# Retention stage: TensorE's order regrouped, rotation's partition swap by DMA, q's row scale in the clip bounds

## The reference

```
q = xf @ Wq.T;  k = xf @ Wk.T * SCALING;  vr = xf @ Wv.T        # 8 heads of 32
qr = q * cos + rotate_every_two(q) * sin;  kr the same with k
# rotate_every_two: (x0, x1, x2, x3, ..) -> (-x1, x0, -x3, x2, ..)
qk = einsum('bhqd,bhkd->bhqk', qr, kr) * mask[None]
den = clip(abs(qk).sum(-1, keepdims=True), 1.0, 50000.0)
out = einsum('bhqk,bhkd->bhqd', qk / den, vr)
out = (out - mu) / sqrt(var + LN_EPS) * ln_g + ln_b             # over each head's 32 values
out = gelu(out, approximate=False) @ Wo.T
```

## Time and profile before

| | before |
|---|---|
| time, median of 3 runs | 2666.49 us (2666.29 to 2668.53) |
| span of the profiled execution | 2667.7 us (its own time is not recorded apart from its span) |
| retention stage within it | about 0 to 1157 us, in which PE is busy 99 to 100% between 170 and 1050 us |
| attention, experts | about 1157 to 1554 us, 1554 to 2668 us |
| DVE, ACT in the stage | about 75% and 60% busy |

### The profile page before, as it was taken

How to read it: one execution, slowest core, us unless ns; L and a number is a source line. 1 busy time by engine, 2 the same in 40 slices (tenths; PEclk the granted TensorE clock), 3 DMA queues, 4 the chain that set the end, 5 groups by cost and what they waited for, 6 DMA issues and landing times. The chain is left out here.

```text
span 2667.7 us, 43895 instructions
## 1 busy us (share of the span) xinstructions
PE 2586.6 (97%) x15328; PEld 1732.6 (65%) x15328; DVE 1844.4 (69%) x2847; ACT 1459.4 (55%) x2044; POOL 517.1 (19%) x444
## 2 busy tenths in 40 slices
PE   5999999999999999969999969999999999999999
PEld 2333343333333434349999958888888888888888
DVE  3877777777777777747777658666666666666665
ACT  2665656565656565635666635555555555555554
POOL 2333333333333333211121210000000000000000
PEclk8999999999999999989999979999999999999999
DMA  6122222222232222121222224000000000000000
GB/s 230 47 77 58 76 68 59 80 55 82 56 84 57 77 58 68 48 85 64 95 94 75 98 90 143 25 25 24 24 24 24 24 24 24 24 24 24 24 17 16
DMA packets 116786, 157.95 MB, mean 59 GB/s; under 512 B 16272, under 2 KB 82328, under 8 KB 116384
## 3 DMA queue, kind: packets, MB, share of 16 engines
q1 hardware_dynamic: 116640, 156.01, 19.7%
HBM read 72.03 MB, written 33.59 MB: 40 GB/s over the span
## 5 line engine op out<-in xcount | busy, mean ns | idle before, releaser
L499 DVE TENSOR_TENSOR l_prod<-l_scores,l_window 128x1024 f32<-128x1024 f32 x512 | 624.0, 1220 | 211.4 <-PE l_scores L325 199.1
L690 ACT ACTIVATE l_absp<-l_prod 128x1024 f32<-128x1024 f32 x512 | 536.5, 1056 | 333.1 <-DVE l_prod L499 331.9
L1707 ACT ACTIVATE e_r<-e_h,e_bn,e_rs 128x512 f32<-128x512 f32 x512 | 399.0, 780 | 484.9 <-PE e_h L1558 480.7
L325 PE MATMUL l_scores<-l_qst,l_kst 96*128 96x512 f32 x1024 | 412.9, 484 | 15.4 <-DMA l_qst<-l_lo 11.6
L325 PEld LDWEIGHTS l_scores<-l_qst,l_kst 96*128 96x128 f32 x1024 | 168.1, 191 | 240.2 <-issue 180.2
L1558 PE MATMUL e_y<-e_whi,e_h2lo 128*128 128x256 f32 x1024 | 289.8, 283 | 0.0
L1557 PE MATMUL e_y<-e_wlo,e_h2hi 128*128 128x256 f32 x1024 | 289.7, 283 | 0.0
L1556 PE MATMUL e_y<-e_whi,e_h2hi 128*128 128x256 f32 x1024 | 289.2, 282 | 0.1
L339 PE MATMUL l_num<-l_prod,l_v 128*32 128x512 f32 x2048 | 273.5, 605 | 0.0
L350 PE MATMUL l_den<-l_absp,l_ones 128*32 128x512 f32 x2048 | 272.7, 604 | 0.0
L1802 DVE CAST e_h1hi<-e_r 128x512 fp32r<-128x512 f32 x256 | 111.2, 434 | 224.3 <-ACT e_r L1707 220.2
(11 more groups left out here) (191 smaller groups left out, 4447.0 us busy)
## 6 DMA issues: line engine op xcount, KB each, us to landing
l_kst<-l_hi SPq DMA_DIRECT2D x256, 64.0 KB, 2.0
l_qst<-l_hi SPq DMA_DIRECT2D x256, 64.0 KB, 2.0
l_raw<-in_xT SPq DMA_DIRECT2D x8, 1024.0 KB, 5.3
l_kst<-l_lo SPq DMA_DIRECT2D x128, 64.0 KB, 2.0
l_qst<-l_lo SPq DMA_DIRECT2D x128, 64.0 KB, 2.0
l_xo<-in_x SPq DMA_DIRECT2D x32, 256.0 KB, 2.8
x_scratch<-l_xo SPq DMA_DIRECT2D x32, 256.0 KB, 2.2
l_xr<-x_scratch SPq DMA_DIRECT2D x8, 1024.0 KB, 8.0
```

The lines of the kernel that those rows point to most:

```text
L325: mm = nc.tensor.matmul(sc[j][:, s, :], kst[g][0:96, h, 128 * kt:128 * kt + 128], qst[c][0:96, h, :], start=True, stop=True)
L499: nc.vector.tensor_tensor(prod[n % 4][:], sc[j][:], win[:, 4 * g + 2 * j:4 * g + 2 * j + 2, w0:w0 + QC], ALU.mult).then_inc(prod_ready, 1)
L690: nc.scalar.activation(absp[n % 4][:], prod[n % 4][:], ACT.Abs).then_inc(abs_ready, 1)
L1707: nc.scalar.activation(r[m][:], p[m][:], ACT.Relu, bias=bn_[layer][1][:, m, e:e + 1], scale=rs[layer][:, m, e:e + 1]).then_inc(done, 1)
```

## The change

1. **PE's order.** A step was: scores pair 0, `sums(i - 1)`, tasks of part 0, scores pair 1, `weighted(i)`, tasks of part 1. It becomes: pair 0, tasks 0, pair 1, tasks 1, `sums(i - 1)`, `weighted(i)`. The matmuls are the same ones.
2. **The swap.** DVE's 64 shuffles go. SP copies `t1` to `t2` with the partitions swapped, by two DMAs of 64 partitions by 2 KB each (`swap_pairs`), which stand ahead of each stack in SP's list. `rotate_sin` (DVE) and `rotate_cos` (POOL) wait for both to have landed.
3. **The row factor of q** is left out of q; the denominator's clip bounds 1 and 50000 are divided by it instead (a table `bounds`, one value per token and head), and `take_den` on DVE becomes two small operations (max, then min). PE waits for the first of them where it waited for the one.
4. **q out of PSUM by ACT** (`take`, at kt = 1 behind ACT's absolutes), not by DVE.

```diff
+            def swap_pairs(n):
+
+                sp.wait_ge(t1_ready, n + 1)
+                for d in range(2):
+                    sp.dma_start(t2[d:128:2, :], t1[1 - d:128:2, :]).then_inc(shuffled, 16)
...
                 if not first:
                     store_x(0, b - 1, 0, 4 * b - 3)
                     load_x(0, b - 1, QC, 16 * (2 * b - 1))
+                swap_pairs(prep_order("q0", b))
                 stack(prep_order("q0", b), qst[1][:, :, :], QUADS["q"], q_stacked)
                 if not first:
                     store_x(1, b - 1, 256, 4 * b - 2)
                     load_x(1, b - 1, QC + 256, 16 * (2 * b - 1))
+                swap_pairs(prep_order("k0", b))
                 stack(prep_order("k0", b), kst[1][:, :, 0:QC], QUADS["k"], k_stacked[0])
...
                 if not last:
+                    swap_pairs(prep_order("k2", b))
                     stack(prep_order("k2", b), kst[0][:, :, 0:QC], QUADS["k"], k_stacked[0])
                 for n in range(2):
                     load_x(n, b, 256 * n, None if first else 32 * b)
                 if not last:
+                    swap_pairs(prep_order("q3", b))
                     stack(prep_order("q3", b), qst[0][:, :, :], QUADS["q"], q_stacked)
...
                     if more:
                         scores(nb, ni, 0)
+                    tasks(0)
+                    if more:
+                        scores(nb, ni, 1)
+                    tasks(1)
                     if i > 0:
                         sums(b, i - 1, first)
                     elif not first:
                         sums(b - 1, STEPS - 1, False)
...
-                    if more:
-                        scores(nb, ni, 1)
                     weighted(b, i, first)
...
-            def q_rotate_in(n, a, g, c):
...
             def rotate_sin(n, c):
 
-                dve.wait_ge(shuffled, n + 1)
+                dve.wait_ge(shuffled, SHUFFLE * (n + 1))
...
-                nc.vector.tensor_scalar(dent[:], nT_A[:, :, 0], 1.0, 50000.0, ALU.max, ALU.min).then_inc(den_ready, 1)
+                nc.vector.tensor_tensor(dent[:], nT_A[:, :, 0], bounds[:, 0, p, :], ALU.max).then_inc(den_floor, 1)
+                dve.wait_ge(den_floor, phase + 1)
+                nc.vector.tensor_tensor(dent[:], dent[:], bounds[:, 1, p, :], ALU.min).then_inc(den_ready, 1)
...
+                    if kt == 1 and (p < 3 or not last):
+                        take(prep_order(f"q{p}", b), A(f"q{p}"), 1.0)
```

More of the change, by code:

```diff
@@ L18, with layer0 @@
 F32R = mybir.dt.float32r
-def layer0(nc, x, xT, wqT, wkT, wvT, woT, lng, lnb, window, rowscale, cosT, sinT, avg8, ident, x1):
+def layer0(nc, x, xT, wqT, wkT, wvT, woT, lng, lnb, window, clip, cosT, sinT, avg8, ident, x1):
     B, L, E = x.shape
@@ L76, in layer0 @@
         win = sb("window", [128, H, (2 * ROWS - 4) * 32])
-        rsc = sb("rowscale", [128, 2, ROWS])
+        bounds = sb("clip", [128, 2, PHASES, 16])
         cos_sb, sin_sb = sb("cos", [128, L]), sb("sin", [128, L])
@@ L144, in _ @@
                 sp.dma_start(dst, src).then_inc(weights_in, 16)
-            for dst, src in ((sin_sb[:], sinT), (cos_sb[:], cosT), (rsc[:], rowscale)):
+            for dst, src in ((sin_sb[:], sinT), (cos_sb[:], cosT), (bounds[:], clip)):
                 sp.dma_start(dst, src).then_inc(tables_in, 16)
@@ L242, in a_free @@
                 else:
-                    pe.wait_ge(den_ready, 4 * b if before == "dT3'" else 4 * b + int(before[2]) + 1)
+                    pe.wait_ge(den_floor, 4 * b if before == "dT3'" else 4 * b + int(before[2]) + 1)
             def b_free(name, b, first, last):
@@ L410, in body @@
[L410 to L419, removed]
@@ L431, in body @@
[L431 to L439, removed]
@@ L440, in body @@
[L440 to L447, removed]
+                    weighted(b, i, first)
@@ L600, in body @@
                     products(b, i, 0, first)
-                    if kt == 2 and prep_q:
-                        shuffle(nq)
                     if kt == 3 and post:
-                        take_den(A("dT" + tag))
+                        take_den(A("dT" + tag), ph, 3 if prev else p - 1)
                         head_sums(Bn("nT" + tag))
-                    if kt == (7 if p == 2 else 6) and prep_k:
-                        shuffle(nk)
                     if not last:
@@ L655, in _ @@
             centre(4 * B - 1)
-            take_den(a_order("dT3'", B - 1, False, "after"))
+            take_den(a_order("dT3'", B - 1, False, "after"), 4 * B - 1, 3)
             variance(4 * B - 1)
@@ L663, in _, with take @@
         def _(act):
-            def k_take(n, a):
+            def take(n, a, scale):
                 if not isinstance(n, int) or n > 0:
@@ L669, in k_take @@
                 act.wait_ge(a_ready, a + 1)
-                nc.scalar.activation(t1[:], pA[:], ACT.Copy, scale=SCALING).then_inc(t1_ready, 1)
+                nc.scalar.activation(t1[:], pA[:], ACT.Copy, scale=scale).then_inc(t1_ready, 1)
             def high(n, before, count):
@@ L746, in body @@
                         if kt == (6 if p == 2 else 5):
-                            k_take(prep_order(f"k{p}", b), A(f"k{p}"))
+                            take(prep_order(f"k{p}", b), A(f"k{p}"), SCALING)
                         if kt == 7:
@@ L1903, in shape_constants @@
     window = gamma[None, :, None, None] ** dist * factor[None, :, None, :]
-    rowscale = np.stack([factor[4 * g + np.arange(128) // 32] for g in range(2)], 1)
+    tok, t, head = np.arange(128)[:, None, None], np.arange(4)[None, :, None], np.arange(4)[None, None, :]
+    scale = np.stack([factor[4 * (p // 2) + head, (512 * (p % 2) + 128 * t + tok) // R].reshape(128, 16) for p in range(4)], 1)
+    clip = np.stack([1.0 / scale, 50000.0 / scale], 1)
     angle = np.repeat(1.0 / 10000.0 ** np.linspace(0.0, 1.0, 16), 2)
@@ L1910, in shape_constants @@
     out = {
-        "window": window.reshape(128, H, -1), "rowscale": rowscale, "cosT": np.tile(np.cos(turn), (4, 1)),
+        "window": window.reshape(128, H, -1), "clip": clip, "cosT": np.tile(np.cos(turn), (4, 1)),
         "sinT": np.tile(sine, (4, 1)), "avg8": np.kron(np.eye(16), np.full((8, 8), 1 / 8)), "ident": np.eye(128),
```

81 lines of the change are left out of this document (43 added, 38 removed).

## The result

The changed kernel takes 2824.83 us (median of 4 runs, 2818.30 to 2828.81) against 2667.51 for the kernel before on the same chip (4 runs, 2666.29 to 2669.76): a ratio of 1.0585, 95% interval 1.0567 to 1.0603, so 157 us slower. The profiled execution has a span of 2821.1 us. PE's last transposes of the retention stage start at 1310.99 us where they started at 1157.15, and from there to the end it is 1510.1 us (before 1510.6), so 153.8 us were lost in the retention stage.

The account below looks back on a forecast made before the run. PE, busy 129.7 of 130 us, was taken to bound the retention stage. Savings of 84 us against waits, start and clock loss summed to +126 on 2667.7, giving 2794; the forecast median was 2792 us, range 2700 to 2860.

Parts of the forecast that it names:

- PE's order with DVE's small waits: Retention stage: fewer changes between full array and narrow groups save 84 us over 256 steps; DVE's extra work returns 12.
- parts 3 and 4: Row factor in the clip bounds and q's exit by ACT: worth nothing by themselves, since DVE is not the bound.
- q3: Phase 3: q3's swap waits behind k2's stack and two loads on SP, costing 7.6 us in seven batches, +53.
- q0 and k0: Phase 0: swaps wait on SP behind stack, loads, store and its wait; q0 +55 (bounds 35 and 65), k0 +12.
- q1, q2, k1 to k3: Other swaps landing late: +14 us for q1 and q2, +4 for k1, k2, k3 and batch 0.
- start: Stage start: swaps and stacks go in series, and batch 0's q0 swap stands behind loads: +12 us (bounds 6 and 18).
- the clock, at q3 and q0: PE's clock halves after long idle waits, 3.4 us on each of 14 waits: +48 us (bounds 0 and 70).
- The step 2.99: PE's step without tasks in the retention stage shrinks from 3.32 to 2.99 us, saving 0.33 each.
- The give-back: DVE's variance, statistics or normalising exceeds its 0.4 us margin, 0.4 us on each of 32 phases: +12 (bounds 0 and 25).
- L + 4.1: PE may start pair 1 of its step 3 4.1 us after L, the swap's landing, once DVE's operations are done.
- the row of 64 KB: Profile row: 2.0 us from a DMA's issue to landing for 64 KB, used for the swap's 128 KB DMAs.
- Rival (a): The stalls come but PE's clock stays up: the forecast without the clock's 48 us, 2744 us; chance 0.25.

Follow-up runs that it names:

- e1: The kernel before with only PE's new order; shuffle, q's exit by DVE and the row factor stay: 2622.60 us, ratio 0.9835.
- e3: The changed kernel with the shuffle kept on DVE, so all of the change but the swap by DMA: 2639.90 us, ratio 0.9895.
- e6: The kernel before with PE's new order and the clip bounds (two-operation `take_den`); shuffle and q's exit on DVE: 2623.65 us, ratio 0.9828.
- e5: The changed kernel with q's exit from PSUM back on DVE at its old place, swap still by SP: 2805.56 us, ratio 1.0513.
- e7: The changed kernel with q0's and q3's swaps moved earlier in SP's list, ahead of loads, store or stack: 2747.94 us, ratio 1.0299.
- e8: The changed kernel with 24 more zero-weight matmuls keeping PE busy in the long waits of phases 3 and 0: 2801.79 us, ratio 1.0493.
- e11: The changed kernel with 48 two-column zero-weight matmuls in phase 0 alone, shifting PE's later instructions by 96: 2813.93 us, ratio 1.0541.
- the best placement: The changed kernel with q's exit on DVE, part 1's tasks last in a step, and q0's, k0's and q3's swaps first: 2700.66 us, ratio 1.0121.

## Why the prediction was right, and where it was not

The forecast was 2792 in a range of 2700 to 2860, and its main chain is shown: SP works in order, q3's and q0's swaps stand behind stacks, loads and a store, DVE waits, then PE. Of the +154 of the stage, its terms measured are:

| term of the sum | forecast | measured, and from what |
|---|---|---|
| PE's order with DVE's small waits | -72 | -45 (e1) |
| parts 3 and 4 | 0 | +17 (e3 less e1) |
| q3 | +53 | 56: phase 3 is 8.0 longer than in e3, 64 over eight, less 8 of the clock |
| q0 and k0 | +67 | 52: phase 0 is 8.8 longer, 62 over seven, less 9 to 10 of the clock |
| q1, q2, k1 to k3 | +18 | 40: phases 1 and 2 are 4.1 and 0.9 longer, eight of each |
| start | +12 | 16 (92.1 less 76.2) |
| the clock, at q3 and q0 | +48 | at most about 17 |
| sum | +126 | about +153 |

**The step 2.99** was exact, and the 0.33 per step real: the narrow groups do lose their extra time beside each other. The Trainium skill, "TensorEngine Tiling (Array Packing)", section "Key Properties", says that changing the tiling mode drains TensorE; the trace agrees, with 0.33 to 0.34 us for each pair of changes taken away. **The give-back** was put down to DVE's variance and statistics, 12 us. It was 39: group means and phase 3's transposes, which wait for `pA` now ahead of the narrow groups (some 17 and 9), and the loop's jump (some 8), read from e1's steps; the rest is spread. I had moved those tasks without asking what they wait for.

**Part 4** was costed at nothing, and there a step failed. I reckoned `t1` ready at 7.0 and it was at 7.5 (650.1 in a phase that began at 642.66), which is near, but I did not ask who wants `pA` next. The transposes of `den` do, and wait in each phase:

```profile
649.56 0.58 ACT L655 ACTIVATE l_t<-l_bankA 128x512 f32<-128x512 f32 x1
```

```profile
650.20 0.66 PE L309 MATMUL l_bankA<-l_ident,l_tB 128*128 128x128 f32 x4 [1.19 <-ACT l_t L655]
```

The step is 4.75 in place of 3.86 in phases 0 to 2, and 5.26 in place of 5.13 in phase 3. e3 less e1 is 17 us and e3 less e6 16. e5's 19 are no third witness, since 15 of them lie in phase 1 beside a fetch that is gone. **The second operation of `take_den`** was put at 0.2 us, in a step where PE has other work. It takes 1.1 to 1.3 in 30 of 32 phases, because POOL's addition runs beside it once the rotation is late (last section), and it stands on the path from the swap to PE, between the sine product and the product that frees pair 1:

```profile
661.79 1.26 DVE L515 TENSOR_TENSOR l_den_t<-l_den_t,l_clip 128x16 f32<-128x16 f32 x1
```

```profile
664.84 1.22 PE L343 MATMUL l_scores<-l_qst,l_kst 96*128 96x512 f32 x2 [0.18 <-DVE l_prod L491]
```

I had put PE's pair 1 at L + 4.1, and it is at L + 5.0 (659.84 to 664.84), in all seven phases 3. That is 0.9 us more on a wait than forecast; no run in the new order has the late swap and this operation at its 0.18 us, so what it costs by itself is not shown.

**q3 and q0**: the forecast landed q3's swap 16.5 us into the phase; it landed at 17.2 (659.84 less 642.66). e7 shows the places in SP's list as the cause. For q0 and k0 the forecast was too high: in batches 1 to 6 the step of q0's wait is 7.8 us longer than in e3 and k0's 1.1, so about 45 us with the clock off where I had 55, and 8 where I had 12.

**q1 and k1**: my 2.05 us for a landing holds where nothing comes between, in e8 and e11 to the tenth; with a fetch of instructions in between it is 3.4 to 4.2. Without the fetch phase 1 is 3.0 us shorter, 24 in all, and the rest of this term, about 16, is near its forecast of 18. So the row of 64 KB was a fair measure of 128 KB, the 2.3 us set beside it in the prediction was 0.2 too high, and the 2.4 in the changed kernel's profile is a median over disturbed and undisturbed ones.

**The clock** was the term most wrong. Half-clock stretches are there as foretold (661.7 to 668.5 at 0.66), but they cost little, since DVE has four products and more to catch up and holds PE anyway: pair 1 starts 5.0 us behind the sine product at half clock here, and at full clock in e7 and e8 too. From the sine product to the next `weighted` are 7.42 us in every undisturbed place at full clock (q3 in e7), 8.5 on average at q3 and 8.7 at q0 after the change: 1.1 and 1.3 us each, not 3.4. Even that is an upper value, since e8 took most of the half clock away and phases 0 and 3 hardly changed. That the sum came near is in part luck: five terms (PE's order, parts 3 and 4, q3, the small waits, the start) were together 73 us too low, and two (q0 and k0, the clock) 46 too high. Rival (a), 2744, was the better on the clock and worse in the sum.

## What to carry to other kernels

Before a copy is handed from an engine that has slack to a queue that works in order, write down what stands ahead of it in that queue at each place: 0.75 us of DVE work a time, on an engine with slack, became 90 us in all in the best placement and 185 in this one. When work changes its order or its engine, ask not only when it is ready but which buffer it holds, who wants that next, and what is queued behind that one. Where PE has stood still and its clock is low, count only the part of its slower work that the engine it waits for would not have cost anyhow.

## What the runs showed of the hardware that I had not expected

A fetch of instructions shares the DMA engines with the data: one 16 KB packet takes 0.9 to 1.9 us on one of them, and rows of the swap wait behind it (e8). In the change 21 of 60 swaps had one in flight beside them, and all but one of these landed 3.1 to 4.3 us after the second DMA's issue; the other 39 took 2.1 to 2.7. In e7, e8 and e11 it is the same: without a fetch at most 2.8, with one 2.9 to 5.0 in 45 of 50. Where it falls hangs on how many instructions stand ahead, so adding 96 of them moved the time of a phase elsewhere by 3 us.

DVE and POOL hold each other up on SBUF. DVE and POOL in phase 1 after the change:

```profile
422.79 0.17 DVE L513 TENSOR_TENSOR l_den_t<-l_bankA,l_clip 128x16 f32<-128x16 f32 x1
422.99 1.28 DVE L515 TENSOR_TENSOR l_den_t<-l_den_t,l_clip 128x16 f32<-128x16 f32 x1
```

```profile
422.96 1.28 POOL L771 TENSOR_TENSOR l_t<-l_t 128x512 f32<-128x512 f32 x1
```

The max, with an operand in PSUM, takes 0.17 us; the min, of the same size with both in SBUF, ends only when POOL's addition ends. In e6, where POOL is not at work then, the min takes 0.18. The Trainium skill, "SBUF — State Buffer", section "SBUF: two separate sides", has an exclusive lock for a DVE operation with two SBUF inputs against GpSimd's; the trace agrees. POOL's cosine product likewise takes 1.785 us after the change, where it starts 0.04 us behind DVE's sine product, which takes 0.69. Before, it started 0.9 to 1.1 us ahead and took 1.287, and the sine product took 0.86.
